# Masked attention on one core: no transposing DMA for the probabilities, a wider exchange, three row buffers, one adjacency tile

## The reference

```
h     = relu((x - mean(x)) / sqrt(var(x) + 1e-5))               # x: 6144 x 128
score = (h @ weight) @ input.T                                  # 6144 x 6144
score = where(adj > 0, score, -2**32 + 1)                       # adj: 6144 x 6144 int32
out   = x + softmax(score / 0.07, axis=1) @ input               # 6144 x 128
```

## Time and profile before

| what | us |
|---|---|
| median of 3 runs (lowest, highest) | 1130.97 (1128.85, 1132.66) |
| the profiled execution, own time | 1126.94 |
| its span, first to last instruction | 1124.8 |
| PE, PE weight loads, busy | 890.8, 593.3 |
| DVE, POOL, ACT busy | 799.4, 737.4, 682.6 |
| granted TensorE clock, mean | 0.979 of full |

### The profile page before, as it was taken

One profiled execution on the slowest core, in us unless ns is written; L12 is line 12 of the kernel. 1 busy time (PEld: TensorE's weight loads), 2 busy tenths in 40 slices (PEclk: granted clock), 3 DMA queues, 4 the chain that ended last, 5 costly groups with the idle time before them and its releaser, 6 DMA issues.

```text
span 1124.8 us, 23907 instructions
## 1 busy us (share of the span) xinstructions
PE 890.8 (79%) x6990; PEld 593.3 (53%) x6990; DVE 799.4 (71%) x1430; ACT 682.6 (61%) x1040; POOL 737.4 (66%) x729
## 2 busy tenths in 40 slices
PE   7767788888877887788788778877888787788875
PEld 4345555555545555555555555555555555555554
DVE  6856667767777776777777776767776777677662
ACT  5546565567556656665675666566656755675663
POOL 4965567757766775676577666756765776577534
PEclk9989999999999999999999999999999999999989
DMA  9498889989999999999999988999988999899943
GB/s 336 135 274 229 232 248 267 267 238 272 280 250 240 283 267 249 264 275 261 239 278 272 251 248 260 276 247 258 283 245 242 264 279 257 239 282 269 216 107 88
DMA packets 249768, 280.23 MB, mean 249 GB/s; under 512 B 182032, under 2 KB 206736, under 8 KB 231312
## 3 DMA queue, kind: packets, MB, share of 16 engines
q1 hardware_dynamic: 242544, 276.65, 88.3%
q10 hardware_dynamic: 7200, 3.28, 1.5%
HBM read 160.50 MB, written 3.15 MB: 145 GB/s over the span
## 4 chain that ended last, share of the span: by engine, by line
SPq 46%; DMA 14%; issue 12%; PE 11%; DVE 10%; POOL 2%; ACT 0%; DVEq 0%; POOLq 0%; ACTq 0%
SPq L350 38%; DMA pT_dma<-split 12%; SPq L365 5%; PE ps_s L856 5%; PE ps_o L886 4%; DVE squares_own L686 4%; DVE nodes_raw L686 4%; SPq L404 2%; PE ps_o L889 2%; POOL nodes_raw L470 1%; DMA adj_i<-in_adj_dram 1%; DVE probs L654 1%; DMA probs<-nodes_raw 1%; DVE chunk_max L654 0%; ACT nodes_raw L551 0%
## 5 line engine op out<-in xcount | busy, mean ns | idle before, releaser
L470 POOL TENSOR_TENSOR nodes_raw<-probs,nodes_raw 128x512 f16<-128x512 f32 x288 | 326.3, 1162 | 314.0 <-ACT nodes_raw L551 314.0
L654 DVE CUSTOM_DVE_ANT_0 probs<-ps_s,adj_i 128x1024 f32<-128x1024 f32 x288 | 351.3, 1220 | 96.5 <-PE ps_s L856 53.2
L856 PE MATMUL ps_s<-yT_hi,hT 128*128 128x512 f16 x1152 | 395.0, 384 | 7.0 <-DVE chunk_max L654 7.0
L565 ACT ACTIVATE pT_hi<-ps_t 128x512 f16<-128x512 f32 x144 | 86.0, 597 | 399.2 <-PE ps_t L877 399.2
L452 POOL TENSOR_SCALAR adj_i<-adj_i 128x2048 uint32<-128x2048 int32 x144 | 271.0, 1909 | 19.7 <-DMA adj_i<-in_adj_dram 19.7
L886 PE MATMUL ps_o<-v,pT_dma 128*128 128x256 f16 x576 | 114.7, 280 | 202.3 <-DMA pT_dma<-split 172.6
L856 PE MATMUL ps_s<-yT_lo,hT 128*128 128x512 f16 x576 | 221.7, 385 | 0.0
L669 DVE TENSOR_TENSOR pT_lo<-ps_t,pT_hi 128x512 f16<-128x512 f32 x144 | 99.1, 688 | 169.9 <-ACT pT_hi L565 169.9
L886 PE MATMUL ps_o<-v,nodes_raw 128*128 128x256 f16 x1152 | 206.2, 273 | 0.9 <-POOL nodes_raw L470 0.8
L886 PEld LDWEIGHTS ps_o<-v,pT_dma 128*128 128x128 f16 x576 | 56.8, 99 | 275.9 <-DMA pT_dma<-split 217.8
L889 PE MATMUL ps_o<-v,nodes_raw 128*128 128x128 f16 x1152 | 198.1, 219 | 0.0
(11 more groups left out here) (78 smaller groups left out, 1031.5 us busy)
## 6 DMA issues: line engine op xcount, KB each, us to landing
adj_i<-in_adj_dram SPq DMA_DIRECT2D x144, 1024.0 KB, 7.2
probs<-squares_own SPq DMA_DIRECT2D x384, 96.0 KB, 3.4
probs<-nodes_raw SPq DMA_DIRECT2D x384, 96.0 KB, 3.5
nodes_raw<-in_L_gnn_input_dram SPq DMA_DIRECT2D x6, 512.0 KB, 7.3
x_res<-in_x_dram SPq DMA_DIRECT2D x48, 64.0 KB, 1.8
out_dram<-fin ACTq DMA_DIRECT2D x48, 64.0 KB, 3.3
x_ln<-in_x_dram SPq DMA_DIRECT2D x46, 64.0 KB, 4.9
pT_dma<-split SPq DMA_TRANSPOSE x144, 3.1
```

The costliest lines, as they stand in the source:

```text
L470: nc.gpsimd.tensor_tensor(lo, exchanged_part(s, m, 1), hi, ALU.subtract).then_inc(lo_e_done, 1)
L654: nc.vector.tensor_tensor_reduce(out=probs[:, s, j * SCORE:(j + 1) * SCORE], in0=ps_s[j % 2][:, :], in1=codes(s, c)[:, part * SCORE:(part ...
L856: made = nc.tensor.matmul(ps_s[j % 2][:, q * 512:(q + 1) * 512], hT[:, s, part, :], y[:, cols], start=(part == 0 and y is yT_hi), stop=(pa ...
```

## The change

The three D turns are gone, with `split`, `pT_dma` and their DMAs. P turns are four (0 to 3), E turns eight (4 to 11), exchanged in four parts of two turns: exp, squares and `hi_e` go by 1024 columns, four instructions each per tile, and each of the sixteen exchanges moves 4096 bytes per partition as four runs of 1024 bytes, where it moved one run of 3072. `probs` has three rows, `adj_i` one buffer: chunk c of tile u is loaded once the two masks of chunk c of tile u-1 are done (adjacency 1 goes to `probs` row 2). Masks of tile t+2 all lie in step t. Products of the last four E turns of a tile and `lo_e` of its last two move into the next step. The loop body holds six steps (tiles 3 to 38), the last nine are unrolled. The core of the diff:

```diff
-    D_TURNS = 3
-    P_TURNS = 3
-    E_TURNS = 6
+    P_TURNS = 4
+    E_TURNS = TURNS - P_TURNS
-    D_BANK = (2, 1, 2)
-    P_BANK = (0, 1, 0)
-    E_SUMS = 2
+    P_BANK = (0, 1, 2, 0)
+    E_SUMS = E_PARTS
+    EARLY_E = 4
+    PROBS = 3
-    TAIL = 5
+    TAIL = 9
+    UNROLL = 6
...
# SP
+            def next_adj(u, c):
+                before = 2 if isinstance(u, int) and u == 2 else 1
+                sp.wait_ge(masked, u * SCORES + (PER_CONV * (c + 1) - before * SCORES))
+                load_adj(u, c)
...
-                        sp.dma_start(probs[b * QUAD:(b + 1) * QUAD, s, first:first + E_COLS // QUADS],
-                                     squares[s][a * QUAD:(a + 1) * QUAD, b, :, :].rearrange("j k i -> j (k i)"))\
+                        to = probs[b * QUAD:(b + 1) * QUAD, r, columns(E_FIRST, E_TURNS)]
+                        sp.dma_start(to.rearrange("j (c a x) -> j c a x", a=QUADS, c=E_PARTS)[:, :, a, :],
+                                     squares[s][a * QUAD:(a + 1) * QUAD, b, :, :].rearrange("j (c k) i -> j c (k i)", c=E_PARTS))\
...
             def step(t, par, r, at):
-                turn_d(t, 2)
+                if has(at, 2) and at != 0:
+                    next_adj(t + 2, 2)
...              # load_x(t + 4), then
+                    next_adj(t + 3, 0)
...              # transpose of h, then
                     exchange_ready(t + 1)
-                    exchange(nxt, range(0, 3))
-                    turn_d(t + 1, 1)
-                    exchange(nxt, range(3, QUADS))
+                    exchange(nxt, (r + 1) % PROBS, range(0, 2))
+                if has(at, 3):
+                    next_adj(t + 3, 1)
+                if has(at, 1):
+                    exchange(nxt, (r + 1) % PROBS, range(2, QUADS))
...
# POOL
             def step(t, par, r, at):
+                if at != 0:
+                    for m in range(E_TURNS - E_PART, E_TURNS):
+                        lo_e(t - 1, (r - 1) % PROBS, m)
-                    convert(t + 2, par, 2)
+                    convert(t + 2, 1)
...              # make_h, split_h, then
+                    convert(t + 2, 2)
-                for m in range(E_TURNS):
-                    lo_e(t, par, m)
+                for m in range(E_TURNS - E_PART):
+                    lo_e(t, r, m)
-                    convert(t + 3, nxt, 0)
-                    convert(t + 3, nxt, 1)
+                    convert(t + 3, 0)
...
# ACT, order of a step after the change
+                    for c in range(3):
+                        exp_e(t + 1, nxt, n, c)
+                for q in range(2):
+                    hi_p(t, q, at)
...              # store of t - 1
+                    exp_e(t + 1, nxt, n, 3)
+                hi_e(t, par, r, 0, at)
+                for q in range(2, P_TURNS):
+                    hi_p(t, q, at)
+                for c in range(1, E_PARTS):
+                    hi_e(t, par, r, c, at)
+                    exp_p(t + 1, nxt, n)
...
# DVE, order of a step after the change (next_mask: tile t + 2, next_squares: tile t + 1)
+                next_mask(0)
+                next_squares(0)
+                next_mask(1)
                     finish(t - 1, nxt, at is None or at > 2)
+                next_squares(1)
                 lo_p(t, 0)
                 lo_p(t, 1)
+                next_mask(2)
+                next_squares(2)
                 lo_p(t, 2)
+                lo_p(t, 3)
+                next_mask(3)
+                next_squares(3)
+                next_mask(4)
                 invert_sum(t, par)
                     x_stats(t + 4, par)
+                next_mask(5)
+                    find_max(t + 2, par)
...
# PE, order of a step after the change
+                for j in range(2):
+                    scores(t, par, j, at)
+                        for m in range(EARLY_E + 2 * j, EARLY_E + 2 * j + 2):
+                            product_e(t - 1, m, None if at is None else at - 1)
+                for j in range(2, 4):
+                    for q in range(2 * j - 4, 2 * j - 2):
+                        turn(t, r, q, at)
+                    scores(t, par, j, at)
+                    if j == 2 and at != 0:
+                        pe.wait_ge(fin_done, t)
+                    for q in range(2 * j - 4, 2 * j - 2):
+                        product_p(t, q, at)
+                for j in range(4, SCORES):
+                    scores(t, par, j, at)
+                    for m in range(2 * j - 8, 2 * j - 6):
+                        product_e(t, m, at)
```

More of the change, by code:

```diff
@@ L161, in gnn_masked_attention_kernel @@
         nodesT = probs[:, 1, :]
[L164 to L170, removed]
+        w, wT, spread_w, spread_nodes = [squares_own[:, i, 0:PER_TURN, :].rearrange("q k i -> q (k i)") for i in range(QUADS)]
+        freed = nodes_raw[:, :, :].rearrange("q b d -> q (b d)")
+        squares = [squares_own, freed[:, 0:E_COLS].rearrange("q (b k i) -> q b k i", b=QUADS, i=QUAD)]
+        pT_e = [pT_e_hi[:, :], freed[:, E_COLS:E_COLS + E_COLS // 2].bitcast(fp16)]
+        V_SQUARES = -(-E_COLS // (PART * D))
         ps_s = [pb(f"ps_s{i}", [P, SCORE], fp32) for i in range(2)]
@@ L256, in h_turns, with split_count, exchanged_part @@
             return u * 8 + (8 * s - 16)
[L258 to L274, removed]
+        def split_count(t, q):
+            return t * P_TURNS + (q + 1)
         def columns(turn, turns=1):
             return slice(turn * TURN, (turn + turns) * TURN)
-        def exchanged_part(s, first, turns):
-            part = probs[:, s, columns(E_FIRST, E_TURNS)].rearrange("q (a k i) -> q a k i", a=QUADS, i=QUAD)
-            return part[:, :, first * PER_TURN:(first + turns) * PER_TURN, :]
+        def exchanged_part(r, c):
+            return probs[:, r, columns(E_FIRST + E_PART * c, E_PART)].rearrange("q (a k i) -> q a k i", a=QUADS, i=QUAD)
         def e_halves(half, first, turns):
@@ L292, in exchanges, with adjacency, codes @@
             return u * 128 + (256 - 128 * s)
[L294 to L300, removed]
+        def adjacency(u, c):
+            if isinstance(u, int) and u == 1:
+                return probs[:, 2, c * CONV:(c + 1) * CONV].bitcast(int32)
+            return adj_i[:, c, :]
+        def codes(u, c):
+            return adjacency(u, c).bitcast(uint32)
         def has(at, ahead):
@@ L307, in steps @@
             for t in range(HEAD):
[L308 to L311, removed]
+                step(t, t % 2, t % PROBS, t)
+            with eng.Fori(HEAD, TILES - TAIL, UNROLL) as i:
+                for k in range(HEAD, HEAD + UNROLL):
+                    step(i + (k - HEAD) if k > HEAD else i, k % 2, k % PROBS, None)
             for t in range(TILES - TAIL, TILES):
-                step(t, t % 2, t)
+                step(t, t % 2, t % PROBS, t)
         block = ctx.enter_context(nc.Block())
@@ L356, in exchange_ready, with step @@
                 sp.sem_inc(sp_waited, 1)
[L358 to L369, removed]
             exchange_ready(0)
[L371 to L375, removed]
+            exchange(0, 0, range(QUADS))
+            def step(t, par, r, at):
                 nxt = 1 - par
-                turn_d(t, 2)
-                if has(at, 3):
-                    next_adj(t + 3, nxt, 1)
+                if has(at, 2) and at != 0:
+                    next_adj(t + 2, 2)
                 if has(at, 4):
@@ L475, in _ @@
                 for c in range(CONVS):
-                    convert(u, u, c)
+                    convert(u, c)
             v_lo_pool(0)
@@ L522, in d_bank @@
[L522 to L535, removed]
@@ L537, in hi_d, with hi_e @@
-            def hi_d(u, q):
-                act.wait_ge(exp_d_done, u * D_TURNS + (q + 1))
-                if not (isinstance(u, int) and u == 0):
-                    act.wait_ge(turned_in[q], u * 16)
-                nc.scalar.activation(split[:, q, 0, :], d_bank(q), ACT.Copy).then_inc(hi_done, 1)
-            def hi_e(u, s, c, at):
+                                     accum_out=chunk_sum[:, s, 1 + c:2 + c]).then_inc(exp_e_done, 1)
+            def hi_e(u, s, r, c, at):
                 act.wait_ge(exchanged[s], exchanges(u, s))
-                if at == 0:
-                    act.wait_ge(v_lo_pool_done, PARTS - 1)
-                else:
+                if at != 0:
@@ L802, in _, with step, next_mask, next_squares @@
-            mask(1, 1, 3)
-            mask(1, 1, 4)
-            def step(t, par, at):
-                nxt = 1 - par
+            mask(1, 1, 1, 0)
+            mask(1, 1, 1, 1)
+            x_stats(3, 1)
+            for c in range(E_PARTS):
+                turn_squares(0, 0, 0, c)
+                mask(1, 1, 1, 2 + c)
+            find_max(1, 1)
+            def step(t, par, r, at):
+                nxt = 1 - par
+                n, m = (r + 1) % PROBS, (r + 2) % PROBS
+                def next_mask(j):
+                    if has(at, 2):
+                        mask(t + 2, par, m, j)
+                def next_squares(c):
+                    if has(at, 1):
```

(17 more changed lines are left out.)

238 lines of the change are left out of this document (82 added, 156 removed).

## The result

The changed kernel took 1136.01 us (median of 20 runs, 1128.36 to 1143.31), the kernel before in runs beside it 1130.91. The ratio is 1.0048, interval 1.0028 to 1.0069: slower by half a per cent, where 2.1% faster was forecast. The profiled execution has a span of 1131.7 against 1124.8. Two of all the executions behind this document lie more than 1.5% above the fastest of their kernel (4563.1 in c3_adj1_first, whose cause nothing here shows, and 1133.87 in b3_before_four), and the ratios leave them out.

What follows compares the result with a forecast made beforehand. The prediction took latency to bind: adjacency chunk 2 behind sixteen exchanges, then POOL, 16.2 + 5.4 = 21.65 us a step. 47 steps plus start and end gave a 1100.8 us span, 1107 as median (2.1% faster); range 1055 to 1165.

Steps and rivals of the forecast that it cites:

- The price of p: SP's queue: p is what issuing one exchange of four runs costs, taken as 0.68 us against 0.63 for one run.
- Rival 1: SP's queue: the sixteen exchanges become dearer and SP binds; loses from p = 0.745, 1161 us at 0.80; chance 0.29.
- Rival 4: Hardware loop: the six-step body no longer stays with the engines, some 3.4 us a return, up to 20 us; chance 0.07.
- Loop 1: One step: sixteen exchanges, the last one's landing, then ACT and DVE work to the square turn; 10.0 + 16p, 20.1 at p = 0.63.
- loop 2: Two steps: adjacency chunk 2 issued behind sixteen exchanges, then POOL, PE and DVE; 16.2 + 8p a step, 21.25 at p = 0.63.
- The sentence on a landing 1 us later: Last exchange: landing 1 us later would grow Loop 1 by 1, to 21.9, and just pass loop 2.
- T: Time of one step, forecast as 16.2 + 5.4 = 21.65 us; break-even at 22.16.
- The sum: Whole kernel: 82.4 + 1017.6 - 6.6 + 2.4 + 5 = 1100.8 us span, 1103 own time, 1107 median.
- The sums per engine: Work per step: POOL fullest at 18.5 us with waits, DVE about 17.7, PE about 17.5, ACT 13.5; none the bound.

Runs made afterwards that it cites:

- c3_adj1_first: a4 with SP issuing adjacency chunk 1 of tile t+3 ahead of all the exchanges, not in their middle; 1038.65 us, ratio 0.9183 to the kernel before.
- b3_before_four: The kernel before with four steps in the loop body in place of two; 1126.85 us, ratio 0.9956.
- a4: The changed kernel written out without a loop, each exchange moving one run of 4096 bytes per partition; 1092.29 us, ratio 0.9663 to the kernel before.
- a1: The changed kernel with all 48 steps written out and no hardware loop; 1102.37 us, ratio 0.9736 to the kernel before.
- a2: The kernel before with six steps in the loop body in place of two; 1188.78 us, ratio 1.0489.
- b1: a4 with SP issuing adjacency chunk 2 of tile t+3 in front of the last four exchanges; 1245.14 us, ratio 1.1003 to the kernel before.
- b4: a4 with the last eight exchanges of each tile issued by ACT's queue; 1140.38 us, ratio 1.0075 to the kernel before.

## Why the prediction was wrong

- **The price of p: nearly right, a little low.** Taken as 0.68, it measured 0.72 on average: 0.64 for an undisturbed exchange, 0.75 on average for the eight behind the chunk of adjacency. Rival 1 (0.745 and more) did not happen. Its "against", that the number of runs is not what makes an exchange dear, held in the main: with one run in place of four a4 still has 0.68.
- **Rival 4 happened, and was undersized.** This is the step that failed: the prediction gave the return of a six-step loop a chance of 0.07 and at most 20 us, and put it at nothing in its sum. It happened at every return, and cost 34 us (a1), the five returns 6 to 7 each, against 3.4. The working counted one fetch and its latency; the profile shows two waits of 3 and 4 us, the other engines starved after them, and TensorE at its lower clock (0.50) for 5 us. The Trainium skill, "Runtime: NRT & Kernel Launch", "Instruction fetch mechanics", on a taken branch out of the held window, was borne out by a2, where each pass fetches again and the time is 1188.78. The window of two pages that the section gives is not what was held on TensorE here: b3's body of four steps has some 1160 matmuls and weight loads (13980 in 48 tiles), over twice the 512 instructions of two such pages, and went round without a loss. The profile of before, whose loop fetched nothing, could not give the size, but the number of steps in the body was in the diff. This step alone turned the sign.
- **Loop 1 binds, not loop 2.** With p = 0.72 the prediction's form for loop 2 gives 16.2 + 5.8 = 22.0, next to the measured 21.91, but that is luck, for the step does not run along that loop. In the written-out kernel (a1) the chain has the landing of an exchange 25 times between 300 and 900 us and that of adjacency once, and in b1 chunk 2 issued earlier made the step longer. The term that was mis-sized is the landing of the last exchange in loop 1: 3.5 was the median of all exchanges, but the last one stands behind the megabyte of adjacency issued in their middle, and, where it is on the chain, landed after 4.1 to 6.3, median 5.1. One turn of loop 1 can be read off the chain shown above, from 561.79 to 583.78: 5.0 for the landing (forecast 3.5), 5.3 from there to the end of the square turn (forecast 5.4), 11.7 for SP's issues (forecast 11.9 at p = 0.68), together 22.0, where the forecast's terms make 20.9. The sentence on a landing 1 us later named this and I did not follow it. b1, with two megabytes ahead, and c3, with none among the exchanges, move the time the way this says. The chain of the looped kernel has such a landing in only 12 steps of that stretch; what ends last in the others was not followed.
- **The sum.** With T = 21.91 the forecast's own sum is 1107 + 47 x 0.26 = 1119; the returns add 34: 1153. Measured 1136. Of the 17 between, 7.7 lie in the last three intervals (20.2, 14.9 and 16.3, 51.4 in place of 3 x 21.91 - 6.6 = 59.1), 3.0 in the long start (the first seven intervals are 2.0, not 5, over 7 x 21.91), 1.4 in the spread (the median is 2.6 above the profiled execution, not 4.0), 1.2 in the first `finish` (81.2, not 82.4), and 3.4 in that the returns of the profiled execution come to 30.6. So it was luck that the range held the time, and luck too that a1 (1102) stands so near 1107: a longer step was set off by a shorter end.
- **The sums per engine.** None of them bound the step, as forecast, and POOL rose by the two `lo_e`. But POOL did not become the fullest engine: it is busy 844.2/48 = 17.6 a step, TensorE 930.1/48 = 19.4. The forecast had 17.5 for TensorE, although with one more turn make 17.67 + 0.4. Its 17.7 for DVE is not the sum of its terms either (16.24 - 1.2 + 1.4 = 16.4); measured is 790.5/48 = 16.5.
- **Right.** That the transposing DMA leaves the chain, that TensorE's extra turn is hidden, and that the step itself gets no longer. It hardly gets shorter either. Without returns the changed kernel (a1) is 2.6% faster than before, and of the 21.6 us between the two profiled spans only 7.5 lie in the 37 steps from tile 7 to 44 (0.2 each); 9.5 lie in the last three intervals (51.5 against 61.0) and 4.5 in the start.

## What to carry to other kernels

When a diff lengthens a hardware loop's body, count the body against what the engine has been seen to hold, before any step is costed: fetches in the middle of the old trace are nought until the edge, and after it each pass pays. When a landing is a term of a loop, take it from the transfer that stands last in its batch, with what is queued in front of it, and not from the median of its kind; and when many small transfers gate a loop, put the large one ahead of them, where its wait allows it. When an issue has to be priced, take its mean over the step and not the undisturbed one: 0.64 and 0.72 here.

## What was not expected of the hardware

- Code that is streamed costs time even with no branch: the kernel before is some 20 us slower written out (1152.01 against 1130.2), with fetches as the only new traffic in view; a4 is some 7 us slower by TensorE's part (1092.29 against 1085.68).
- A body of four steps was held on TensorE, one of six was not (5 and 49 fetches on q8 in 800 us; 40 with no loop).
- An undisturbed exchange of four runs of 1024 bytes is issued almost as fast as one of a single run of 3072 (0.64 and 0.63), but with a megabyte of adjacency issued among them the sixteen took 0.72 each on average, and single ones up to 1.9.
- Eight of sixteen exchanges moved to a second queue made the kernel 48 us slower (b4 against a4); adjacency then landed after 9.2 in place of 6.8, for a reason that no run isolates.
